# Attention with residual and layer norm: one copy moved to an earlier round, and transposes put ahead of scores where a quad begins

## The reference

```python
q = (x @ Wq.T).reshape(B, N, NUM_HEADS, HEAD)
k = (x @ Wk.T).reshape(B, N, NUM_HEADS, HEAD)
v = (x @ Wv.T + bv).reshape(B, N, NUM_HEADS, HEAD)
a = jnp.einsum('bnhd,bmhd->bhnm', q, k) * SCALE + encoding_bias[:, None, :, :]
pad_mask = jnp.all(a == 0, axis=-1)
a = jnp.where(pad_mask[..., None], -jnp.inf, a)
a = jnp.nan_to_num(jax.nn.softmax(a, axis=-1))
o = jnp.einsum('bhnm,bmhd->bnhd', a, v).reshape(B, N, HIDDEN)
return _layernorm(x + o @ Wo.T + bo)
```

## Time and profile before

| | before |
|---|---|
| median of three runs, us | 1248.02 (1247.92 to 1248.37) |
| profiled execution, us | 1248.19 |
| its span from first to last instruction, us | 1246.4 |
| granted TensorE clock, mean | 0.998 of full |
| TensorE matmuls busy | 1218.8 us, 98% |
| VectorE busy | 1054.4 us, 85% |
| ScalarE busy | 1017.0 us, 82% |
| GpSimd busy | 866.7 us, 70% |
| HBM traffic over the span | 70 GB/s |

### The profile page before, as it was taken

How to read it: one execution, slowest core, us unless ns; L and a number is a source line. 1 busy time by engine, 2 the same in 40 slices (tenths; PEclk the granted TensorE clock), 3 DMA queues, 4 the chain that set the end, 5 groups by cost and what they waited for, 6 DMA issues and landing times.

```text
span 1246.4 us, 34374 instructions
## 1 busy us (share of the span) xinstructions
PE 1218.8 (98%) x11796; PEld 1057.3 (85%) x11796; DVE 1054.4 (85%) x5094; ACT 1017.0 (82%) x4007; POOL 866.7 (70%) x775
## 2 busy tenths in 40 slices
PE   8999999999999999999999999999999999999996
PEld 7888888888888888888888888888888888888885
DVE  5788888888888888888888888888888888888986
ACT  6888888888888878888887888788888888887874
POOL 1777777677677777777776777677777767776774
PEclk9999999999999999999999999999999999999999
DMA  6022211222121222112221212221122212122100
GB/s 232 22 72 86 79 55 54 82 75 80 56 77 61 72 86 80 54 54 83 74 79 61 80 55 71 86 79 54 58 83 71 80 62 79 54 71 86 54 28 26
DMA packets 58895, 88.85 MB, mean 71 GB/s; under 512 B 3680, under 2 KB 54624, under 8 KB 58720
## 3 DMA queue, kind: packets, MB, share of 16 engines
q1 hardware_dynamic: 58720, 86.65, 21.4%
HBM read 61.47 MB, written 25.17 MB: 70 GB/s over the span
## 4 chain that ended last, share of the span: by engine, by line
PE 77%; ACT 19%; DVE 2%; issue 1%; POOL 1%; DMA 0%; POOLq 0%; SPq 0%; DVEq 0%
PE turn_bank L208 17%; PE turn_bank L210 17%; PE turn_bank L209 17%; PE pT_bank L256 12%; ACT probs L496 11%; PE score_bank L244 9%; PE turn_bank L268 6%; ACT pT L503 4%; ACT qkT L484 2%; ACT xT_hi L472 1%; DVE neg_a L624 0%; DVE out_sb L688 0%; DMA xT_raw<-xT_dram 0%; POOL inv_std L779 0%; POOL probs L772 0%
## 5 line engine op out<-in xcount | busy, mean ns | idle before, releaser
L496 ACT ACTIVATE probs<-neg_a,neg_max 128x128 f32<-128x128 f32 x1536 | 596.1, 397 | 3.7 <-DVE neg_max L624 3.5
L772 POOL TENSOR_TENSOR probs<-probs,row_scale 128x768 f32<-128x768 f32 x256 | 376.7, 1471 | 199.8 <-DVE row_scale L652 199.8
L765 POOL TENSOR_TENSOR fold<-neg_a 128x384 f32<-128x384 f32 x256 | 282.9, 1105 | 124.5 <-DVE neg_max L624 124.4
L624 DVE CUSTOM_DVE_ANT_0 neg_a<-score_bank,adj_sb 128x128 f32<-128x128 f32 x1536 | 333.4, 287 | 0.1
L503 ACT ACTIVATE pT<-pT_bank 128x384 f32<-128x384 f32 x512 | 220.7, 484 | 102.9 <-PE pT_bank L256 102.8
L496 ACT ACTIVATION_READ_ACCUMULATOR probs<-neg_a,neg_max 128x1 f32 x1536 | 302.5, 197 | 0.0
L208 PE MATMUL turn_bank<-xT_hi,w_hi 128*128 128x512 f32 (+1 forms) x594 | 240.9, 406 | 2.3 <-DVE w_lo L606 2.3
L210 PE MATMUL turn_bank<-xT_hi,w_lo 128*128 128x512 f32 (+1 forms) x594 | 231.7, 390 | 0.0
L209 PE MATMUL turn_bank<-xT_lo,w_hi 128*128 128x512 f32 (+1 forms) x594 | 230.6, 388 | 0.0
L256 PE MATMUL pT_bank<-ident,probs 128*128 128x128 f32 x1536 | 217.1, 278 | 0.3 <-ACT pT L503 0.3
L256 PEld LDWEIGHTS pT_bank<-ident,probs 128*128 128x128 f32 x1536 | 173.8, 141 | 21.1 <-issue 1.1
(11 more groups left out here) (39 smaller groups left out, 1961.9 us busy)
## 6 DMA issues: line engine op xcount, KB each, us to landing
xT_raw<-xT_dram SPq DMA_DIRECT2D x32, 768.0 KB, 4.7
x_sb<-x_dram SPq DMA_DIRECT2D x32, 768.0 KB, 4.7
out_dram<-out_sb SPq DMA_DIRECT2D x128, 192.0 KB, 1.9
adj_sb<-adj_dram SPq DMA_DIRECT2D x32, 256.0 KB, 3.2
w_raw<-wq_t_dram SPq DMA_DIRECT2D x1, 576.0 KB, 5.7
w_raw<-wk_t_dram SPq DMA_DIRECT2D x1, 576.0 KB, 6.8
w_raw<-wv_t_dram SPq DMA_DIRECT2D x1, 576.0 KB, 7.8
w_raw<-wo_t_dram SPq DMA_DIRECT2D x1, 576.0 KB, 8.4
```

Source lines behind the costliest of these rows:

```text
L496: last = nc.scalar.activation(probs[t % 2][:, u, :], neg_a[t % 2][:, u, :], ACT.Exp, bias=neg_max[t % 2][:, u:u + 1], scale=-1.0, accum_ou ...
L624: last = nc.vector.tensor_tensor_reduce(out=neg_a[t % 2][:, u, :], in0=score_bank[trio][:, c * N:(c + 1) * N], in1=adj_sb[q % 2][:, b, :], ...
L765: nc.gpsimd.tensor_tensor(fold[:, u, :], neg_a[t % 2][:, u, 0:N // 2], neg_a[t % 2][:, u, N // 2:N], ALU.add).then_inc(fold_done, 1)
L772: nc.gpsimd.tensor_tensor(probs[t % 2][:, u, :], probs[t % 2][:, u, :], row_scale[:, u].unsqueeze(2).broadcast_to([P, HALF, N]), ALU.mult) ...
```

## The change

On TensorE, in the first round of second_half, transpose_probs(t + 3, 0) moves from behind scores(t + 4) to between attend(t + 2) and the wait for the sixth q/k copy. The wait and the scores follow it, and the v product follows the scores. On ScalarE the copy of chunk 1 of xT_hi of the quad after next moves from the middle of round b = 1 to the end of round b = 0, right behind the copy of chunk 0. No instruction is added or taken away.

```diff
@@ -313,9 +313,9 @@
 
                 wait_y_read(t + 1)
                 attend(t + 2)
+                transpose_probs(t + 3, 0)
                 pe.wait_ge(qk_done, kn + 6)
                 scores(t + 4)
-                transpose_probs(t + 3, 0)
                 project_v(t + 4, 0)
                 project_out(t + 2)
                 transpose_probs(t + 3, 1)
@@ -536,8 +536,6 @@
                     keep_qk(LAST, 0, turn)
                 if t == TAIL + 5:
                     keep_qk(LAST, 4, turn)
-                if b == 1 and has_after:
-                    keep_xT_hi(q + 2, 1)
                 if more2:
                     exp_trio(t + 2, 2)
                 if more:
@@ -548,6 +546,7 @@
                 if b == 0 and has_after:
                     act.wait_ge(v_psum, t + 4)
                     keep_xT_hi(q + 2, 0)
+                    keep_xT_hi(q + 2, 1)
                 if b == 1 and not tail:
                     keep_qk(q + 1, 5, turn)
                 if b == 3 and not tail:
```

## The result

The changed kernel is slower: 1251.85 us against 1247.92, medians of seven runs each, a ratio of 1.0024 (1.0014 to 1.0035). The same kernel timed again, beside the later experiments, gave 1250.73 against 1248.58, a ratio of 1.0016 (1.0008 to 1.0025). I had forecast 1245.5 and a range up to 1248.4.

What follows compares the result with a forecast made beforehand. TensorE, busy 98%, was taken to bound the kernel, with a 0.30 us stall a quad. The new order gains 0.10, less 0.01 new wait: 29 × 0.09 = 2.6 us, giving 1245.5 us, range 1242.0 to 1248.4.

Steps and rivals of the forecast that it cites:

- The bound: TensorE, busy 98% of the span, sets the time; it falls only where TensorE stands still or runs a dearer order.
- the stall of 0.30: First round of second_half: scores wait for ScalarE's copy of the last q/k block, 0.30 us a quad.
- ScalarE's edit: Moving the second xT_hi copy a round earlier costs nothing; the last q/k copy begins some 0.33 earlier.
- The price of the order: TensorE, opening round: attention to transposes 0.79, to scores 0.80, to v product 0.88; gain 0.10 a round, not 0.30.
- What is late next: Later scores delay VectorE's bias and first v copy by 0.11; the second v product waits 0.01, leaving 0.09 gain.
- the lag from scores to bias: VectorE's bias begins 0.96 after scores start, so at 628.58 in the opening round instead of 628.47.
- a margin of 0.01: Second v product: released by the v copy at 632.32, TensorE there at 632.31, a new wait of 0.01.
- the slower one: VectorE holds the second v product: with a bias lag of 1.35, 0.30 lost a round, 1256.7 us; chance 0.07.
- The rival of an equal price: Transposes to scores at 0.91, or v copy 0.08 later: gain 0 to 0.03 a round, 1247.2 to 1248.2; chance 0.12.
- The two limits practically meet: At the second v product, the v copy's release (632.32) and TensorE's own arrival (632.31) nearly coincide; gain left 0.09.

Runs made afterwards that it cites:

- The runs with either order and nothing late: Kernel before with all xT_hi copies at the end of round b = 0 and no xT_lo copy in the opening round: old TensorE order 1239.52 us, new order 1245.11.

## Why the prediction was wrong

**The bound** was right: TensorE's list sets the time, and the stall of 0.30 sat where the views said. It went: of the 31 waits of scores on this q/k copy among the weight loads' waits, 2 are left, none in one of the 29 opening rounds that were changed.

**ScalarE's edit** was right in each number: 0.49 of idle time left, the q/k copy at once behind its product, scores without a stall in the old order.

**The price of the order** was right: 0.79, 0.81 and 0.88 against 0.79, 0.80 and 0.88, and the 0.74 of the earlier trace rows held as a price for transposes followed by scores. The runs with either order and nothing late put the new order at 0.19 a round above the old one without its stall; the prediction had 0.30 − 0.10 = 0.20. The Trainium skill, "TensorEngine Tiling (Array Packing)", section "Key Properties", says that changing the tiling mode drains TensorE; that an order with one such change more takes longer agrees with it.

**"What is late next" failed**, and in it one term: the lag from scores to bias. I took 0.96 from the earlier trace rows. It was 1.08. The row came from the last rounds, where the bias step waits for scores alone; in the opening round it is the first step of a quad and waits for the bias matrix too, a term that the sum did not have. Of the 0.12 between them 0.11 is the second wait, as the run with that wait moved shows. Put on a step that I had given a margin of 0.01, it is all wait: the v copy let the second v product start 6.42 behind attention and not 6.29. Another 0.03 came from small terms of the same sum: with the lag at 0.97 the second v product still came at 6.32, and the round was 10.18 long (625.76 to 635.94). So even with the right lag the gain would have been 0.05 a round, about 1.3 us, and not 2.6. Of the 4.9 us between the gain of 2.6 that was forecast and the loss of 2.3 in the rounds, the lag is 29 × 0.11 = 3.2, the small terms some 1.2, and the two long rounds 0.4. The sum had no such rounds; in the run with the wait moved, four of them left a gain of 0.5 us over the whole stretch (55.59 to 1157.94).

**The rival that came** was the slower one: VectorE holds the second v product. Its place and its point were right (it decides from a lag of 1.05 on), its size was not (I had worked it at 1.35), and 0.07 was too small a chance for a limit that by my own sum stood 0.09 from deciding. I had called 0.96 a lag and 1.35 a queue, and had not asked whether the step in the opening round has the same waits as the step in the row. The rival of an equal price was worked out wrongly as well: with 0.91 for the transposes scores come 0.11 later too, the bias at 628.69, and the v copy lets the second v product start at 632.43. That is a loss of 0.02 a round, or 1248.6, and not a gain of 0 to 0.03.

**The chances** leaned on the forecast as if its two limits were known apart. "The two limits practically meet" should have given the cases on both sides about the same weight.

**The comparison that I passed over:** the prediction says that the ScalarE edit alone would let scores start without a stall. Then the new order could only cost, since it trades 0.30 of stall that is already gone for 0.19 of price and scores that are later by 0.80. The runs show it: 1244.0 with the one edit, 1250.7 with both.

## What to carry to other kernels

When two edits aim at the same stall, price each alone first: the second may find nothing left to remove and still charge its own cost. When an edit makes a step later that feeds another engine, follow that engine's list to the next bank or buffer that the first engine wants back; here a gain of 0.10 ended at a copy six steps on. Before a lag is read from another place of the trace, check that the instruction there has the same waits: here one wait more made it 0.11 longer.

## What the hardware showed that I had not expected

**A second wait can cost though it is met:** where VectorE stood waiting for scores, its bias step started 1.07 or 1.08 behind them with two waits (all 29 rounds of the changed kernel) and 0.96 or 0.97 with one (27 of 29 rounds). Where VectorE came late from its own list, the second wait cost nothing. Why it costs was not tried.

**VectorE and GpSimd stretch each other:** of an xT_lo copy and a fold that overlap, the one that starts second pays, 1.25 instead of 0.69 or 1.39 instead of 1.01. One exchange of two neighbours in VectorE's list made the changed kernel 12.6 us slower by it: the residual came 0.56 later behind attention (7.71 against 7.15), which is what the xT_lo copy took more.

**TensorE's clock in the last rounds differs between executions of one kernel, and 1 to 2 us of the total go with it.** The stretch from 1225 to 1235 us, columns as busy time of PE, PEld, DVE, ACT and POOL, then the granted clock, DMA share and GB/s, in the traces of before and of after:

```profile
1225.00:1235.00 10.00, 8.44 (x62) 7.77 (x63) 6.59 (x21) 5.45 (x23) 5.81 (x6) 0.83 0.06 22
```

```profile
1225.00:1235.00 10.00, 6.39 (x58) 5.31 (x58) 8.50 (x42) 6.84 (x29) 7.03 (x7) 1.00 0.11 42
```

In the trace of before TensorE stands still for 2.64 us until oT_lo is done (1225.89). Soon after it goes on, its clock falls from the upper level, 2.4 GHz, to 1.2 GHz for a part of that stretch: three matmuls, start to start, take 0.93 (1226.53 to 1227.46) instead of 0.52 (1222.05 to 1222.57). In the first trace of after TensorE stands still as long, and the clock stays full, so the idle time alone does not decide it:

```profile
1228.14 0.44 PE L208 MATMUL turn_bank<-w_hi,oT_hi 128*128 128x384 f32 x1 [2.64 <-DVE oT_lo L660]
```

The changed kernel's executions with a mean clock of 0.998 took 1250.1 to 1250.9 us, those with 0.995 to 0.997 took 1251.7 to 1252.3, and the two with 1.000 took 1249.5. Most of the seven of the first timing were of the lower kind. So of the first difference of 3.9 us, 2.3 are the rounds, and the rest goes with the clock in the last rounds. Why one execution of the same list meets the half clock there and another does not was not tried and stays open.
